# A two-layer transformer kernel: first layer's output bias added by GpSimd, and the written orders arranged anew

## The reference

```python
def reference(x, ...):                                   # x: 8 x 512 x 256
    sa, ca, ga, sb, cb, gb = modulation(silu(L0_c) @ L0_wmod)   # ga, gb: at least 0.25 in size
    h = layernorm(x) * (1 + ca) + sa
    x = x + ga * L0_attn(h)            # L0_attn ends in  out @ W_out.T + b_out
    h = layernorm(x) * (1 + cb) + sb
    x = x + gb * L0_ffn(h)
    ...                                # the same again with layer 1 (no biases)

def L0_attn(h):        # 16 heads of 16, softmax inside blocks of 64 tokens
    qkv = h @ W_qkv.T + b_qkv
    ...
    return out @ W_out.T + b_out

def L0_ffn(h):
    gf = global_net(h.mean(axis=1))    # three small layers
    out = h
    for _ in range(3):                 # each cycle needs the one before
        tf = coupling_net(out)         # 256-256-128-64-1, gelu, sigmoid
        out = out + coupling(gf, tf) * twist(out)
    return out
```

## Time and profile before

| | |
|---|---|
| median of three runs | 2006.01 us |
| profiled execution, its own time | 2008.09 us |
| its span | 2006.5 us, 30524 instructions |
| TensorE | busy 1952.0 us (97%), 11224 matmul instructions |
| TensorE's weight loads | 1318.5 us (66%) |
| VectorE | 1128.3 us (56%) |
| ScalarE | 935.4 us (47%) |
| GpSimd | 693.9 us (35%) |
| DMA | 76.67 MB, mean 38 GB/s |
| chain of work that ended last | PE 89%, DVE 6%, ACT 2%, DMA 1% |

### The profile page before, as it was taken

How to read it: one execution, slowest core, us unless ns; L and a number is a source line. 1 busy time by engine, 2 the same in 40 slices (tenths; PEclk the granted TensorE clock), 3 DMA queues, 4 the chain that set the end, 5 groups by cost and what they waited for, 6 DMA issues and landing times.

```text
span 2006.5 us, 30524 instructions
## 1 busy us (share of the span) xinstructions
PE 1952.0 (97%) x11224; PEld 1318.5 (66%) x11224; DVE 1128.3 (56%) x2912; ACT 935.4 (47%) x2040; POOL 693.9 (35%) x820
## 2 busy tenths in 40 slices
...
DMA packets 59560, 76.67 MB, mean 38 GB/s; under 512 B 7107, under 2 KB 52686, under 8 KB 59158
## 3 DMA queue, kind: packets, MB, share of 16 engines
...
...
## 4 chain that ended last, share of the span: by engine, by line
PE 89%; DVE 6%; ACT 2%; DMA 1%; issue 1%; POOL 0%; SPq 0%; DVEq 0%; POOLq 0%; ACTq 0%
PE bank L740 12%; PE bank L953 11%; PE bank L966 11%; PE bank L803 6%; PE bank L827 4%; PE bank L839 4%; PE bank L858 4%; PE bank L754 3%; PE bank L566 3%; PE bank L725 3%; PE bank L871 3%; PE bank L592 3%; PE bank L812 3%; PE bank L790 2%; PE bank L687 2%; PE bank L634 2%
## 5 line engine op out<-in xcount | busy, mean ns | idle before, releaser
L953 PE MATMUL bank<-xin,ew 128*128 128x256 f32 x1024 | 235.6, 382 | 0.0
L1193 ACT ACTIVATE h<-bank 128x512 f32<-128x512 f32 x128 | 76.0, 597 | 326.1 <-PE bank L953 325.9
L966 PE MATMUL bank<-ew,h 128*128 128x256 f32 x1024 | 227.5, 379 | 0.0
L966 PEld LDWEIGHTS bank<-ew,h 128*128 128x128 f32 x1024 | 194.1, 190 | 27.4 <-issue 1.3
L953 PEld LDWEIGHTS bank<-xin,ew 128*128 128x128 f32 x1024 | 189.2, 190 | 26.3 <-issue 2.7
L1740 POOL TENSOR_TENSOR s<-s,ri 128x256 f32<-128x256 f32 (+3 forms) x128 | 161.0, 1273 | 128.2 <-DVE ri L1508 128.2
L1778 POOL DMA_INDIRECT out<-y,indices x64 | 102.0, 1594 | 285.5 <-DVE y L1645 200.4
L1169 ACT ACTIVATE s<-s,mn 128x128 f32<-128x128 f32 (+3 forms) x256 | 141.0, 551 | 120.8 <-DVE mn L1501 120.6
L1486 DVE SCALAR_TENSOR_TENSOR th<-th,bank 128x384 f32<-128x384 f32 (+1 forms) x192 | 106.1, 595 | 125.3 <-ACT th L1160 125.0
L1645 DVE SCALAR_TENSOR_TENSOR y<-bank,gates,gbe 128x256 f32<-128x256 f32 x64 | 30.8, 483 | 247.9 <-PE bank L966 245.1
L803 PE MATMUL bank<-look,term 128*128 128x384 f32 (+3 forms) x512 | 156.7, 439 | 0.1
...
## 6 DMA issues: line engine op xcount, KB each, us to landing
...
wqkv<-w_qkv SPq DMA_DIRECT2D x1, 3072.0 KB, 10.2
...
```

Of the source, the lines that this page charges most:

```text
L953: mm = te.matmul(banks[i][:, g * 2 * P:(g + 1) * 2 * P], w1[:, kk, (2 * n + g) * P:(2 * n + g + 1) * P], xin[:, kk, :, :].rearrange("p h s ...
L966: mm = te.matmul(banks[i][:, 0:D], ex.h1[:, g, n * P:(n + 1) * P], w2[:, g, :], start=(g == 0), stop=(g == FC - 1))
```

## The change

- The bias is kept as a 128 x 256 tile. `setup0`'s matmul takes the value bias as 128 equal columns, and VectorE adds its result to the loaded b_out once.
- L635 and the three bf16 parts are gone; `out0` has two matmuls a tile.
- A new step `bias0` on GpSimd, once a batch: it waits for the gate row (`ga0_in`) and for `xn` (x has been read by norm:0), multiplies gate row by bias (128 x 256), and adds that to all four token tiles of x (128 x 1024). `out0` on VectorE waits for it instead of for the gate row.
- HEAD now holds the head and what was PERIOD for b = 0; PERIOD runs for b = 1 to 4; LAST begins with what was PERIOD for b = 5. The steps are the same apart from the eight `bias0`. All three tables are in a new order.

```diff
 HEAD = """
...
-    1sc0:5 1cols:0 0w1_load:0 0tp0:6 0pv0:2 1wt0:5 0tp0:7 1sc0:6 1tp0:5 1wt0:6 0pv0:3 1sc0:7 1pv0:2 1wt0:7 0out0:0
-    0out0:1 1tp0:6 0stats:1 0norm:1 1tp0:7 1pv0:3 1out0:0 0feat:1 1out0:1 1stats:1 0cn1:0 0gc:0 0cn2:0 0twist:0
-    1norm:1 0gc:1 0cn3:0 0gc:2 0cn4:0 1feat:1 0cn1:1 1cols:1 0cn2:1 1cn1:0 1rows:0 0tables:0 0cn3:1 1gc:0 0cn4:1
-    1cn2:0 1gc:1 1twist:0 1cn3:0 1gc:2 1cn4:0 0cn1:2 1cn1:1 0cn2:2 1cn2:1 1cn3:1 0cn3:2 1cn4:1 0cn4:2 1cn1:2 1cn2:2
-    0gate0:0 1cn3:2 1cn4:2 1gate0:0 0fin0:0 1fin0:0 0stats:2 1stats:2 0norm:2 1norm:2 0feat:2 1feat:2
...
+    0sc0:7 0tp0:6 0pv0:2 0bias0:0 0wt0:7 1wt0:4 1wt0:5 1cols:1 0tp0:7 1pv0:1 0pv0:3 1sc0:6 1tp0:4 1tp0:5 1sc0:7
+    1wt0:6 1wt0:7 0out0:0 1pv0:2 0out0:1 1tp0:6 0stats:1 1tp0:7 1pv0:3 0norm:1 1out0:0 0feat:1 1out0:1 0cn1:0 0gc:0
+    0cn2:0 0twist:0 0gc:1 0cn3:0 1stats:1 1norm:1 0gc:2 0cn4:0 1feat:1 1gc:0 0cn1:1 0cn2:1 0cn3:1 0cn4:1 0cn1:2
+    1cn1:0 1rows:0 0cn2:2 0cn3:2 1gc:1 0cn4:2 0gate0:0 1gc:2 1cn2:0 0fin0:0 0stats:2 0norm:2 1twist:0 1cn3:0 1cn4:0
+    0feat:2 1cn1:1 2x0:0 0proj:0.0 0proj:0.1 1cn2:1 0proj:0.4 1cn3:1 2stats:0 0proj:0.2 0look:0.0 2norm:0 1cn4:1
+    0proj:0.3 1cn1:2 0look:0.1 0term:0 2ga0_load:0 0turn_vu:0 0tables:0 0vc:0 1cn2:2 2bias0:0 2feat:0 1cn3:2
+    0look:0.2 1cn4:2 2kq:0 0look:0.3 1gate0:0 2kq:1 0w:0.0 1fin0:0 2sc0:0 0vc:1 2sc0:1 2v:0 2wt0:0 2wt0:1 2v:1
...
 PERIOD = """
...
-    proj:2.2 -softmax:0 +gc:1 +cn3:0 w:1.1 +gc:2 +cn4:0 look:2.0 look:2.1 look:2.2 proj:2.4 turn_vu:2 su:5 +cn1:1
-    look:2.3 sw:5 +cn2:1 attend:3 +cn3:1 turn:4 sc:5 term:2 weigh:5 +cn4:1 proj:3.3 +cn1:2 proj:3.2 w:2.0 attend:4
-    su:6 +cn2:2 turn:5 sw:6 -probs:0 +cn3:2 attend:5 o_out:1 sc:6 weigh:6 su:7 w:2.1 sw:7 +cn4:2 proj:3.0 proj:3.1
...
+    proj:0.0 proj:0.4 proj:0.3 +x0:0 +stats:0 +norm:0 -weigh:11 proj:0.2 proj:0.1 +ga0_load:0 +feat:0 -attend:10
+    look:0.0 term:0 look:0.1 look:0.2 look:0.3 +bias0:0 +kq:0 -turn:11 +kq:1 -attend:11 vc:0 +sc0:0 -o_out:3
...
+    +cn2:0 weigh:4 proj:2.2 +gc:1 -softmax:0 +cn3:0 w:1.1 turn:3 +gc:2 +cn4:0 look:2.0 look:2.1 look:2.2 attend:3
+    +cn1:1 proj:2.4 turn_vu:2 su:5 +cn2:1 sw:5 +cn3:1 term:2 look:2.3 sc:5 weigh:5 proj:3.3 turn:4 w:2.0 +cn4:1
+    proj:3.2 su:6 attend:4 turn:5 +cn1:2 sw:6 +cn2:2 w:2.1 +cn3:2 attend:5 o_out:1 sc:6 weigh:6 -probs:0 su:7 sw:7
...
 def all_steps():
     order = list(written(HEAD))
-    for b in range(B - 2):
+    for b in range(1, B - 3):
         order += period(b)
...
             for kk in range(KC):
-                mm = te.matmul(banks[i][0:3, 0:D], b0.bv3[:, kk, :], b0.wout[:, kk, :], start=(kk == 0),
+                mm = te.matmul(banks[i][:, 0:D], f.a1[:, kk, 0:P], b0.wout[:, kk, :], start=(kk == 0),
                                stop=(kk == KC - 1))
...
                 for kk in range(KC):
-                    te.matmul(out, f.aT[:, kk, t * P:(t + 1) * P], b0.wout[:, kk, :], start=(kk == 0), stop=False)
-                mm = te.matmul(out, c_.ones[:, :], b0.bout_parts[:, :], start=False, stop=True)
+                    mm = te.matmul(out, f.aT[:, kk, t * P:(t + 1) * P], b0.wout[:, kk, :], start=(kk == 0),
+                                   stop=(kk == KC - 1))
...
-            v.tensor_tensor(bout, bout, banks[i][0:3, 0:D], ALU.add).then_inc(drained[i], 1)
...
+            v.tensor_tensor(b0.bout[:, :], b0.bout[:, :], banks[i][:, 0:D], ALU.add).then_inc(drained[i], 1)
...
         elif step == "out0":
             if n == 0:
-                v.wait_ge(f.sem["ga0_in"], 16 * (lap + 1))
+                v.wait_ge(f.sem["x0_bias"], 2 * (lap + 1))
...
+        elif step == "bias0":
+            gated = f.a2[:, 0:D]
+            if b < 2:
+                i, nth = at["setup0", 0, 0, 0]
+                g.wait_ge(drained[i], nth)
+            g.wait_ge(f.sem["ga0_in"], 16 * (lap + 1))
+            g.wait_ge(f.sem["xn"], (3 * lap + 1) * NT)
+            g.tensor_tensor(gated, f.ga[:, :], b0.bout[:, :], ALU.mult).then_inc(f.sem["x0_bias"], 1)
+            g.wait_ge(f.sem["x0_bias"], 2 * lap + 1)
+            g.tensor_tensor(f.x[:, :, :], f.x[:, :, :], gated.unsqueeze(1).to_broadcast([P, NT, D]), ALU.add
+                            ).then_inc(f.sem["x0_bias"], 1)
```

More of the change, by code:

```diff
@@ L52 @@
 HEAD = """
[L53 to L57, removed]
@@ L63 @@
+    0attend:5 0o_out:1 0sw:7 0sw:8 0look:3.0 0weigh:6 0proj:3.4 0look:3.1 0look:3.2 0sc:7 0term:3 0look:3.3
+    0turn_vu:3 0turn:6 0sc:8 0w:3.0 0weigh:7 0weigh:8 0attend:6 0su:9 2norm:2 0sw:9 0su:10 0turn:7 0sw:10 0sc:9
+    2feat:2 0attend:7 0turn:8 0w:3.1 0attend:8 0o_out:2 0weigh:9 0sc:10 0weigh:10 0su:11 0turn:9 0sw:11 0sc:11
+    0attend:9 0turn:10
 """
 PERIOD = """
-    -x1_load:0 proj:0.0 +x0:0 +stats:0 proj:0.1 +norm:0 proj:0.3 +ga0_load:0 proj:0.2 proj:0.4 -weigh:11 +feat:0
-    look:0.0 term:0 look:0.1 look:0.2 -attend:10 -turn:11 +kq:0 +kq:1 turn_vu:0 -attend:11 vc:0 +sc0:0 +wt0:0 +sc0:1
@@ L70 @@
-    look:0.3 +sc0:2 vc:1 +tp0:0 w:0.0 +v:0 +v:1 +wt0:1 +wt0:2 +tp0:1 +sc0:3 -o_out:3 +tp0:2 +wt0:3 proj:1.2 +sc0:4
-    +pv0:0 +sc0:5 -out1:0 +wt0:4 +wt0:5 +tp0:3 -out1:1 su:0 proj:1.0 -stats_t:0 sw:0 sc:0 +sc0:6 vc:2 +tp0:4 +tp0:5
-    +wt0:6 +pv0:1 w:0.1 proj:1.1 +sc0:7 vc:3 turn_vu:1 weigh:0 su:1 sw:1 sc:1 +pv0:2 +wt0:7 +tp0:6 weigh:1 proj:1.4
-    turn:0 proj:1.3 -norm_t:0 +tp0:7 su:2 sw:2 look:1.0 look:1.1 +pv0:3 look:1.2 sc:2 term:1 look:1.3 w:1.0 attend:0
-    turn:1 weigh:2 +out0:0 +out0:1 +stats:1 proj:2.1 proj:2.3 su:3 +norm:1 attend:1 sw:3 -feat_t:0 turn:2 +feat:1
@@ L75 @@
-    su:4 proj:2.0 sw:4 sc:3 sc:4 attend:2 +cn1:0 o_out:0 +twist:0 weigh:3 +gc:0 turn:3 -gate:0 +cn2:0 weigh:4
-    proj:2.2 -softmax:0 +gc:1 +cn3:0 w:1.1 +gc:2 +cn4:0 look:2.0 look:2.1 look:2.2 proj:2.4 turn_vu:2 su:5 +cn1:1
-    look:2.3 sw:5 +cn2:1 attend:3 +cn3:1 turn:4 sc:5 term:2 weigh:5 +cn4:1 proj:3.3 +cn1:2 proj:3.2 w:2.0 attend:4
-    su:6 +cn2:2 turn:5 sw:6 -probs:0 +cn3:2 attend:5 o_out:1 sc:6 weigh:6 su:7 w:2.1 sw:7 +cn4:2 proj:3.0 proj:3.1
-    sc:7 look:3.0 turn:6 su:8 +gate0:0 sw:8 look:3.1 turn_vu:3 weigh:7 +fin0:0 look:3.2 sc:8 term:3 look:3.3 weigh:8
```

133 lines of the change are left out of this document (74 added, 59 removed).

## The result

The changed kernel takes 1974.0 us, the median of four runs (1967.0, 1970.6, 1977.3, 1978.6), against 2005.9 beside it: ratio 0.9835, 95% interval 0.9801 to 0.987. The forecast was 1975. The profiled execution is the shortest of the four, 1967.03 us with a span of 1965.8; so its rows show where TensorE still waits, but its clock, 0.997 in the mean over the span, is the best of the four (0.991 to 0.997). The profiled execution of the kernel before has 0.989, the lowest that its executions show (0.989 to 0.994).

What follows compares the result with a forecast made beforehand. TensorE, busy 1952.0 of 2006.5 us, was taken to bound the kernel. Terms -12.2 (bias matmul), -12.5 (head) and -7 (periods) sum to -31.7, forecast 1975 us, range 1959 to 1992.

Steps and rivals of the forecast that it cites:

- The bias matmul goes.: First layer's out0: one L635 matmul fewer in each of 32 token tiles, 0.38 us each, 12.2 us less.
- bias0 comes in on GpSimd: Two GpSimd operations, 2.5 us a batch, 20 us in all, covered by other matmuls: put at nothing.
- The rival in which it blocks VectorE: bias0 holds back VectorE operations up to 2.5 us each with the chain bare: +20, 1995 us; chance 0.04.
- The first period is written into the head.: Head: batch 0's first cn2 to first projection takes 44 instead of 69.0 us; 12.5 us less after work moved and waits.
- PE idle at L601 released by GpSimd: Listed sign that the prediction is wrong: TensorE idle at the tp0 transposes until GpSimd releases it.
- The periods are arranged anew.: Six steady periods: new order takes 7 of 15.6 us of TensorE waits; bounds 0 and 15.6.
- cn2's wait: Each period, 1.2 us at L687: gelu late because L1419 was slowed while L1740 ran on GpSimd; may go or stay.
- the other wait: Each period, 1.3 us: transposes wait for a bank that VectorE (L1486) drains; expected to go in the new order.
- LAST and the set-up: Last periods and bias set-up: zero each; bounds -1.3 and +5 for LAST, at most 1 us either way for set-up.
- More than that: Rival: clock and overlap cost nothing in the head and all period waits go, -46, 1960 us; chance 0.2.
- Only the matmul: Rival: new waits in head and periods as large as the old, only -12.2, 1994 us; chance 0.1.
- The low clock: Rival: TensorE stays at 1.2 GHz through batch 0's chain and the work behind it, 2007 or 2017 us; chance 0.03.

Runs made afterwards that it cites:

- bias_only: The kernel before with only the new bias: no L635 matmul, bias0 on GpSimd put into the old orders; 1996.2 against 2007.5 us, ratio 0.9946.
- twice_bias: The kernel before with each L635 bias matmul issued twice; ratio 1.0028 to the kernel before, +5.6 us.
- no_bias0: The changed kernel without the eight bias0 steps, so the first layer's output bias is not added; 1975.7 us, ratio 0.9828 to the kernel before.
- old_early: The changed kernel with the order of before up to 0out0:0, bias0 and 1cols:1 put in; 1970.7 us, ratio 0.9835 to the kernel before.
- weigh_later: The kernel before with GpSimd's scaling step weigh:5 moved behind cn4:1 and proj:3.2 in PERIOD; ratio 1.0022, +4.4 us.
- all_three: The changed kernel with the early order of before, 1cols:1 late and batch 1's twist ahead of 0fin0; 1971.5 us, ratio 0.9829 to the kernel before.

## Why the prediction was right

**Direction, size and place.** 1975 was said for 1974.0, of three terms: 12.2, 12.5 and 7 were 11, 8 and 13. The sum was better than its parts: the head was 4.5 too large and the periods 6 too small. That these two cancel, to 1 us, is luck; the same code alone runs from 1967 to 1979.

**"The bias matmul goes."** 12.2 against 11 in bias_only, where bias0's wait takes some 1.5 back, and 0.40 a tile in its period where the spacing had said 0.38. The size and the view were right: the start-to-start spacing with and without the matmul, and not the 0.28 of its own row. The lower bound that was given, 0.21, took the matmul to be the price; twice_bias shows 0.12 for one more of them.

**"bias0 comes in on GpSimd ... I put it at nothing."** Right by no_bias0. Its price on the engine was too low, 2.5 a batch; it takes 0.73 + 2.35 = 3.1. The row it was taken from multiplies by a column repeated along the row (L1740); bias0's second operand has a value of its own for each element of a row of 256. The same multiplication of 128x256 takes 0.73 in that form (L1705) and 0.61 with a column (the shortest of L1740). The term's premise, that bias0's place has cover, failed in the old head of bias_only (1.8 us instead of 0.3) and held in the new order. The rival in which it blocks VectorE, with the chain bare, is out for the changed kernel, since taking bias0 away gives nothing back.

**"The first period is written into the head."** The chain by hand was right: 44 was said from the first cn2 to the first projection, it is 45.6, and the work taken out of the stretch, behind it and (1cols:1) ahead of it, is 39.5 - 30.5 = 9.0 at full clock (each stretch less its idle and clock time) where 10.5 was said. Batch 1's chain is covered by the projections. That gives 45.6 + 9.0 instead of 69.0, 14.4, near the 14.5 before the allowance. What failed is what was left out of the sum: the steps before 82 us, which are in a new order too, were put at zero. They cost about 3 us (old_early 1.5 to 2.5 by time, 3.5 by idle), 2.0 of it waits for GpSimd's scaling, the sign that the prediction had listed as "PE idle at L601 released by GpSimd". The rest is the clock: the sum took it from 11.8 to 4, 7.8 less, from one execution of before. In the profiled execution of after 3.8 came; but in others the drop falls elsewhere and costs 10.6 over the head, hardly less than the 12.3 before, and the old head can do with 5.0 (bias_only). So this part of the term is too large in most executions: what is sure of the head is some 3 us of idle time, 5 to 6 against the old head with bias0, and clock time that a denser order seemed to remove was in part only moved.

**"The periods are arranged anew."** 7 of a possible 15.6 was said; it is 13. Both named waits are gone and no new one repeats. The term was mis-sized by caution: "a repeated order can also have a wait that no row of before shows" was true and took half of it, and here it did not happen. The cause of cn2's wait was right: weigh_later shows L1740 as it, and also that moving the one step alone makes a new wait of 1.7; what made the difference is the order around it. That the other wait went for the reason given, other matmuls ahead of the drained bank, fits the trace and was not tested alone.

**LAST and the set-up, zero.** After 1400 us idle is 565.8 - 558.92 = 6.9 against 7.1 in the earlier trace rows. Right.

**The rivals.** "More than that" needed all the waits gone and a head without clock cost; the periods nearly gave that, the head did not. "Only the matmul" is what bias_only measures, 1996. The low clock did not hold: behind the first projection it is 1.00 in the profiled run of after, and in all_three it is 1.00 again from 160 us.

What stays open: when the clock falls. The same code has it from 80 to 90 us and in three periods in one execution and not in another, and no edit tried here removed it from the head; by the clock's sums 6.8 + 3 x 1.7 = 11.9 us, by the spans 11.4, lie between the changed kernel's two profiled executions.
